# Moving one piece of the second feed-forward product ahead of a pair of products with V, and one subtraction up in VectorE's order

## The chip, the cores and the metric

The kernel runs on one core of a Trainium2 chip. A core has TensorE (PE, matmuls), VectorE (DVE), ScalarE (ACT), GpSimd (POOL) and SyncE (SP, which here issues all DMAs of the main loop). Each engine works through its own list of instructions in order and waits on semaphores for the others. The metric is the device time of the whole kernel in microseconds.

## The reference

The input is x with 4 sequences of 2048 tokens and 512 features. Two blocks follow each other, each with a residual:

```
h  = layernorm(x)
xk, xv, xr, xg = h + (h shifted by one token - h) * time_maa_{k,v,r,g}
r, k, v = xr @ Wr.T, xk @ Wk.T, xv @ Wv.T      # 32 heads of 16
g = silu(xg @ Wg.T)
for every chunk of 64 tokens:
    att   = (r @ k) * w_mat                      # 64 x 64 for every head
    y     = att @ v + (r @ state) * wb
    state = ws * state + (k * wk) @ v
x1  = x + (groupnorm(y) * gamma + beta) * g @ Wo.T
out = x1 + (gelu(layernorm(x1) @ W0.T + bias0) @ W1.T + bias1)   # hidden size 2048
```

## The kernel before

A prologue transposes the weights and splits each into a high and a low float16 part. Products of two split operands take three passes (high*high, high*low, low*high). "hi" parts are made by ScalarE as a float16 copy, "lo" parts by subtraction, mostly on VectorE.

The main loop runs over 32 blocks of 256 tokens. One step n of the loop mixes three stages of different blocks, so that TensorE always has something to do: attention of block n (`att_n`), gate, output product Wo and residual of block n-1 (`tail`), and the feed-forward layer of block n-2 (`ff`). The last four pieces of the second feed-forward product of block n-3 (`late`) stand in the next step. `ahead` is the normalizing and mixing of block n+1. Each engine has one function a step (`pe_step`, `dve_step`, `act_step`, `pool_step`, `sp_step`) with the order written out by hand.

The functions that matter here:

- `pe_down(eng, f, j)` (L785) is piece j of eight of the second feed-forward product: 8 matmuls of 128x512 that add into both banks of `F`. It waits for its weights in slot `use % 5` of `ring`, which `sp_weights` (L1291) loads; a load waits until the piece five uses back has been read.
- `pe_att_v(eng, n, t)` (L685) multiplies the attention weights of a pair of chunks with V, 96 small matmuls. It waits for `s_al`, which `dve_weights_lo` (L948) raises. `pe_from_state(eng, n, t)` (L702) follows.
- `pe_scores` (L669) makes the raw weights of chunk c, `dve_weigh` (L942) multiplies them with the decay mask, `act_weights_hi` (L1145) makes the high part, `dve_weights_lo` (L948) the low part.
- `mix_lo(eng, n, m)` (L234) makes the low part of mixed input m: 128x1024 elements, both inputs in SBUF. It waits for `act_mix_hi` (L230).
- `dve_state` (L957 and L971, in the last chunk L959) updates the state S; ScalarE copies it (L1151) and GpSimd makes its low part (L1257).
- `dve_variance` (L885) sums squares; `dve_residual` (L914) adds x to the output product in `B`, after which TensorE may write `B` again (`pe_Wo` for the second half, L753, waits for the first residual).
- `dve_take_y` (L987, L992) takes the pair's result out of the banks that `pe_att_v` and `pe_from_state` filled. `pe_V` (L639) of the next step waits for it and for `mix_lo` of input 2.

Within a step TensorE's order near the change is `pe_Wo` 0, `pe_kv`, `pe_down` 0, `pe_scores` 3, `pe_down` 1, `pe_Wo` 1, `pe_att_v` 1, `pe_from_state` 1, `pe_down` 2 and 3; the next step begins with `pe_K` (L611 into `sc`).

Of the kernel before, what the change touches and what calls it, by code (L numbers as in the profile page):

```python
# [34 lines left out]
def due(count):  # L35

    return not isinstance(count, int) or count > 0
# [29 lines left out]
def rows(t):  # L67
    return slice(P * t, P * t + P)
# [6 lines left out]
def program(nc, ctx, a, consts, x, out, wd, nb):  # L75
# [156 lines left out]
    def mix_lo(eng, n, m):  # L232
        eng.wait_ge(s_mh, 4 * n + m + 1)
        eng.tensor_tensor(mix[:, m % 2, 1, :, :], mixf[:, m % 2, :, :], mix[:, m % 2, 0, :, :],  # L234
                          ALU.subtract).then_inc(s_ml, 1)
# [364 lines left out]
    def in_step(n):  # L600

        return n < nb, 1 <= n <= nb, 2 <= n <= nb + 1, n + 1 < nb, 3 <= n <= nb + 2
# [12 lines left out]
    def pe_mixed(eng, n, m):  # L615
        eng.wait_ge(s_ml, 4 * n + m + 1)
        eng.wait_ge(s_mh, 4 * n + m + 1)

    def pe_K(eng, n, half):
        if due(n):  # L620
            eng.wait_ge(s_am, 8 * (n - 1) + 7 + half)
        pe_project_T(eng, sc[:, half, :], K_, n, 0, half).then_inc(s_pK, 1)
# [118 lines left out]
    def pe_Wo(eng, n, t):  # L741
        p = n - 1
        if t == 0:
            if n < nb:
                eng.wait_ge(s_gT, 2 * n + 2)
            if due(p):
                eng.wait_ge(s_x1, NT * p)
        else:
            eng.wait_ge(s_x1, NT * p + 1)
        eng.wait_ge(s_ygl, NT * p + t + 1)  # L750
        for i, (a, b) in enumerate(PASSES):
            for kk in range(G):
                mm = eng.matmul(B[:, :], yg[:, a, kk, rows(t)], WT[:, O_, b, kk, :],  # L753
                                start=(i == 0 and kk == 0), stop=(i == 2 and kk == G - 1))
        mm.then_inc(s_Wo, 1)
# [20 lines left out]
    def pe_down(eng, f, j):  # L776
        use = UNITS * f + 8 + j
        eng.wait_ge(s_w[use % RING], 16 * (use // RING + 1))
        if j == 0:
            eng.wait_ge(s_h, NH * (f + 1))  # L780
        for i in range(2):
            k = 2 * j + i
            for t in range(NT):
                for a in range(2):
                    mm = eng.matmul(F[:, t, :], hT[:, k, rows(t)], ring[:, use % RING, i, a * C:(a + 1) * C],  # L785
                                    start=(k == 0 and a == 0), stop=(k == NH - 1 and a == 1))
        mm.then_inc(s_dn, 1)

    def pe_step(eng, n):
        att_n, tail, ff, ahead, late = in_step(n)  # L790
        if att_n:
            pe_mixed(eng, n, 0)
            pe_K(eng, n, 0)
        if late:
            pe_down(eng, n - 3, 4)
        if att_n:
            pe_K(eng, n, 1)
        if late:
            pe_down(eng, n - 3, 5)
        if att_n:  # L800
            pe_mixed(eng, n, 1)
            pe_R(eng, n, 0)
        if late:
            pe_down(eng, n - 3, 6)
        if att_n:
            pe_R(eng, n, 1)
        if late:
            pe_down(eng, n - 3, 7)
        if att_n:
            pe_mixed(eng, n, 2)  # L810
            pe_V(eng, n, 0)
        if ff:
            pe_up(eng, n, 0)
        if att_n:
            pe_V(eng, n, 1)
        if ff:
            pe_up(eng, n, 1)
        if tail:
            pe_yT(eng, n)
        if ff:  # L820
            pe_up(eng, n, 2)
        if ahead:
            eng.wait_ge(s_rl, 2 * n + 1)
            pe_X(eng, n + 1, 0)
            eng.wait_ge(s_rl, 2 * n + 2)
            pe_X(eng, n + 1, 1)
        if ff:
            pe_up(eng, n, 3)
        if att_n:
            pe_scores(eng, n, 0)  # L830
            pe_kv(eng, n, 0, ahead)
            pe_G(eng, n, 0, ahead)
        if ff:
            pe_up(eng, n, 4)
        if att_n:
            pe_scores(eng, n, 1)
        if ff:
            pe_up(eng, n, 5)
        if att_n:
            pe_G(eng, n, 1, ahead)  # L840
        if ff:
            pe_up(eng, n, 6)
        if att_n:
            pe_att_v(eng, n, 0)
            pe_from_state(eng, n, 0)
            pe_scores(eng, n, 2)
        if ff:
            pe_up(eng, n, 7)
        if tail:
            pe_Wo(eng, n, 0)  # L850
        if att_n:
            pe_kv(eng, n, 1, ahead)
        if ff:
            pe_down(eng, n - 2, 0)
        if att_n:
            pe_scores(eng, n, 3)
        if ff:
            pe_down(eng, n - 2, 1)
        if tail:
            pe_Wo(eng, n, 1)  # L860
        if att_n:
            pe_att_v(eng, n, 1)
            pe_from_state(eng, n, 1)
        if ff:
            pe_down(eng, n - 2, 2)
            pe_down(eng, n - 2, 3)


# [68 lines left out]
    def dve_weigh(eng, n, c):  # L937
        for x in range(2):
            eng.wait_ge(s_sc, 8 * n + 2 * c + x + 1)
            if due(8 * n + 2 * c - 1 + x):  # L940
                eng.wait_ge(s_al, 8 * n + 2 * c - 1 + x)
            eng.tensor_tensor(att32[:, x, :], sc[:, x, :], wmask[:, 8 * x:8 * x + 8, :].rearrange("p q i -> p (q i)"),  # L942
                              ALU.mult).then_inc(s_am, 1)

    def dve_weights_lo(eng, n, c):
        for x in range(2):
            eng.wait_ge(s_ah, 8 * n + 2 * c + x + 1)
            eng.tensor_tensor(att[:, c % 2, 1, C * x:C * x + C], att32[:, x, :], att[:, c % 2, 0, C * x:C * x + C],  # L948
                              ALU.subtract).then_inc(s_al, 1)
# [70 lines left out]
    def dve_step(eng, n):  # L1020
        att_n, tail, ff, ahead, late = in_step(n)
        if not att_n:
            dve_e(eng, n - 3)
        for k in range(LN_STEPS):
            if ahead:
                dve_ln(eng, n + 1, k)
            if att_n:
                if k < 4:
                    dve_mix(eng, n, 2, k)
                elif k in (6, 13):  # L1030
                    dve_K_lo(eng, n, (6, 13).index(k))
                if 7 <= k < 11:
                    dve_mix(eng, n, 3, k - 7)
            if tail and k < 2 + RSQRT_STEPS + NT:
                dve_normalize(eng, n - 1, k)
        if att_n:
            mix_lo(eng, n, 2)
            dve_R_lo(eng, n, 0)
            dve_R_lo(eng, n, 1)
            if late:  # L1040
                dve_e(eng, n - 3)
            dve_vw(eng, n, 0)
            if ahead:
                dve_carry(eng, n + 1)
            eng.tensor_scalar(wsf[:, :], ws[:, :], flag[:, n + 1:n + 2], None, ALU.mult).then_inc(s_wsf, 1)
            dve_V_lo(eng, n, 0)
            mix_lo(eng, n, 3)
            dve_vw(eng, n, 1)
            dve_V_lo(eng, n, 1)
        if tail:  # L1050
            dve_gated(eng, n - 1)
        if ahead:
            dve_dx(eng, n + 1)
        if att_n:
            dve_weigh(eng, n, 0)
            dve_state(eng, n, 0)
            dve_weights_lo(eng, n, 0)
            dve_gate(eng, n, 0)
            dve_weigh(eng, n, 1)
            if ahead:  # L1060
                for g in range(2):
                    dve_mix(eng, n + 1, 0, g)
            dve_weights_lo(eng, n, 1)
            if ahead:
                for g in range(2, G):
                    dve_mix(eng, n + 1, 0, g)
            dve_state(eng, n, 1)
            if ahead:
                mix_lo(eng, n + 1, 0)
            dve_gate(eng, n, 1)  # L1070
            if ahead:
                for g in range(G):
                    dve_mix(eng, n + 1, 1, g)
            dve_take_y(eng, n, 0)
            dve_weigh(eng, n, 2)
            dve_weights_lo(eng, n, 2)
            dve_variance(eng, n, 0)
        if ahead:
            mix_lo(eng, n + 1, 1)
        if tail:  # L1080
            dve_residual(eng, n - 1, 0)
        if att_n:
            dve_state(eng, n, 2)
            dve_weigh(eng, n, 3)
            dve_weights_lo(eng, n, 3)
            dve_state(eng, n, 3)
        if tail:
            dve_residual(eng, n - 1, 1)
            dve_fln(eng, n - 1)
        if att_n:  # L1090
            dve_take_y(eng, n, 1)
# [376 lines left out]
```

## Time and profile before

| | |
|---|---|
| median of 3 runs | 2341.43 us (2336.86 to 2341.84) |
| profiled execution | 2341.74 us, span of its instructions 2339.9 us |
| mean granted TensorE clock | 0.962 of full |
| busy: TensorE / VectorE / ScalarE / GpSimd | 93% / 80% / 46% / 16% |

In the profile's rows a line such as "L685" is a line of the kernel; "x96" means 96 instructions merged into one row; what stands in square brackets is the idle time of that engine before the row and what ended it. Rows of instructions carry the start and the time in microseconds, counted from the start of the span. Merged rows overlap a little at their ends, since matmuls are pipelined; differences of starts are exact.

### The profile page before, as it was taken

The page shows a single profiled execution, that of the slowest core. Times are in us where ns is not written, and L with a number is a line of the kernel's source. Part 1 is how long each engine was busy: PE and PEld are TensorE (multiplying, and loading weights), DVE is VectorE, ACT ScalarE, POOL GpSimd, SP SyncE. Part 2 cuts the span into 40 slices and gives each one's busy share as a digit, 9 for nine tenths or more (in the row PEclk, how much of TensorE's full clock was granted, in tenths as well). Part 3 has the DMA queues.
Part 4 walks back from the last instruction along what each step waited for, and adds up shares of the span by engine and source line. Part 5 has one row for each costly group of instructions (what it writes and reads, how often), then busy time and mean ns, then how long its engine had stood idle before and what let it go on. Part 6 is the DMA issues. An engine that isn't in the chain of part 4 may idle for free.

```text
span 2339.9 us, 63070 instructions
## 1 busy us (share of the span) xinstructions
PE 2175.4 (93%) x26328; PEld 1567.0 (67%) x26328; DVE 1865.5 (80%) x4326; ACT 1077.9 (46%) x1902; POOL 384.6 (16%) x334
## 2 busy tenths in 40 slices
PE   3567999999999999999999999999999999999998
PEld 3455777766676776667677666777766676776664
DVE  5879888878887887888788788888888888888751
ACT  5533545444444544444454444445444444454441
POOL 0111111111111111111111111111111111111120
PEclk8788999999999999999999999999999999999999
DMA  8531566665556666555676656566665556666566
GB/s 263 193 87 50 164 204 212 196 201 168 180 173 199 213 196 202 166 174 180 199 215 196 195 166 189 184 197 204 196 208 178 178 176 193 203 204 194 171 211 209
DMA packets 281708, 437.83 MB, mean 187 GB/s; under 512 B 124752, under 2 KB 157904, under 8 KB 281424
## 3 DMA queue, kind: packets, MB, share of 16 engines
q1 hardware_dynamic: 276512, 433.31, 59.7%
q8 instruction: 209, 3.42, 0.6%
q10 hardware_dynamic: 4912, 0.48, 0.2%
q14 instruction: 75, 0.61, 0.1%
HBM read 316.27 MB, written 25.17 MB: 146 GB/s over the span
## 4 chain that ended last, share of the span: by engine, by line
PE 62%; DVE 23%; issue 5%; ACT 5%; DMA 1%; SPq 0%; DVEq 0%; POOL 0%; POOLq 0%; ACTq 0%
PE F L785 15%; PE F L771 13%; PE B L611 7%; PE Y L639 7%; PE sc L611 6%; DVE mixf L202 6%; DVE att L948 5%; PE T L611 3%; DVE mix L234 3%; PE Y L685 3%; DVE S L971 3%; ACT hT L1179 2%; DVE kv L957 2%; PE Y L702 2%; ACT att L1145 2%
## 5 line engine op out<-in xcount | busy, mean ns | idle before, releaser
L771 PE MATMUL F<-xT,ring 128*128 128x256 f16 x4096 | 491.2, 274 | 6.5 <-DMA xT<-xh 5.3
L785 PE MATMUL F<-ring,hT 128*128 128x512 f16 x2048 | 493.5, 389 | 1.2 <-ACT hT L1179 1.2
L771 PEld LDWEIGHTS F<-xT,ring 128*128 128x128 f16 x4096 | 397.2, 98 | 69.3 <-issue 8.1
L785 PEld LDWEIGHTS F<-ring,hT 128*128 128x128 f16 x2048 | 197.0, 100 | 218.2 <-issue 27.6
L230 ACT ACTIVATE mix<-mixf 128x1024 f16<-128x1024 f32 x128 | 135.3, 1057 | 378.2 <-DVE mixf L202 194.6
L1179 ACT ACTIVATE hT<-F,b,f_rho 128x256 f16<-128x256 f32 x512 | 260.3, 562 | 45.4 <-PE F L771 45.3
L202 DVE SCALAR_TENSOR_TENSOR mixf<-dx,maa,xnT 128x256 f32<-128x256 f32 x512 | 273.1, 559 | 0.0
L611 PE MATMUL B<-mix,WT 128*128 128x256 f16 x2304 | 269.5, 274 | 1.8 <-DVE gT L978 1.8
L1257 POOL TENSOR_TENSOR Shl<-S,Shl 128x512 f16<-128x512 f32 x128 | 153.9, 1202 | 691.4 <-ACT Shl L1151 691.4
L611 PEld LDWEIGHTS B<-mix,WT 128*128 128x128 f16 x2304 | 223.7, 98 | 37.9 <-DVE gT L978 2.0
L948 DVE TENSOR_TENSOR att<-att 128x512 f16<-128x512 f32 x256 | 179.8, 742 | 50.1 <-ACT att L1145 50.1
L1151 ACT ACTIVATE Shl<-S 128x512 f16<-128x512 f32 x128 | 80.1, 626 | 287.5 <-PE Y L702 145.7
L639 PE MATMUL Y<-WT,mix 128*128 128x512 f16 x768 | 178.9, 384 | 7.6 <-DVE mix L234 7.6
L611 PE MATMUL sc<-mix,WT 128*128 128x256 f16 x1536 | 180.3, 275 | 3.5 <-PEq L455 3.5
L1262 POOL TENSOR_TENSOR x<-e,x 128x512 f32<-128x512 f16 x64 | 73.0, 1161 | 671.8 <-DVE e L1017 671.8
L234 DVE TENSOR_TENSOR mix<-mixf,mix 128x1024 f16<-128x1024 f32 x126 | 181.6, 1441 | 0.0
L942 DVE TENSOR_TENSOR att<-sc,wmask 128x512 f32<-128x512 f32 x256 | 164.2, 683 | 20.7 <-PE sc L669 20.7
L753 PE MATMUL B<-WT,yg 128*128 128x512 f16 x768 | 178.6, 382 | 1.6 <-DVE x L914 1.5
L685 PE MATMUL Y<-vbd,att 128*64 128x32 f16 x6144 | 116.5, 187 | 63.1 <-DVE att L948 63.1
L611 PEld LDWEIGHTS sc<-mix,WT 128*128 128x128 f16 x1536 | 151.3, 99 | 35.0 <-issue 4.0
L685 PEld LDWEIGHTS Y<-vbd,att 128*64 128x64 f16 x6144 | 111.0, 118 | 84.3 <-issue 84.3
L1145 ACT ACTIVATE att<-att 128x512 f16<-128x512 f32 x256 | 148.5, 630 | 20.7 <-DVE att L942 19.6
(153 smaller groups left out, 2947.7 us busy)
## 6 DMA issues: line engine op xcount, KB each, us to landing
ring<-w_dram SPq DMA_DIRECT2D x512, 512.0 KB, 4.1
kx<-kT SPq DMA_DIRECT2D x96, 256.0 KB, 3.7
rx<-rT SPq DMA_DIRECT2D x96, 256.0 KB, 3.4
xa<-in_L_attn_x SPq DMA_DIRECT2D x32, 512.0 KB, 7.3
vbd<-vN SPq DMA_DIRECT2D x256, 64.0 KB, 2.7
x<-in_L_attn_x SPq DMA_DIRECT2D x32, 512.0 KB, 4.9
out<-x SPq DMA_DIRECT2D x32, 512.0 KB, 3.3
raw<-in_L_ffn_W SPq DMA_DIRECT2D x8, 1024.0 KB, 14.4
```

Source lines behind the costliest of these rows:

```text
L202: last = eng.scalar_tensor_tensor(out=mixf[:, m % 2, g, :], in0=dx[:, g, :], scalar=maa[:, m, g:g + 1], in1=xnT[:, g, 1:BT + 1], op0=ALU.m ...
L234: eng.tensor_tensor(mix[:, m % 2, 1, :, :], mixf[:, m % 2, :, :], mix[:, m % 2, 0, :, :], ALU.subtract).then_inc(s_ml, 1)
L611: mm = eng.matmul(out[:, gg * BT:(gg + 1) * BT], WT[:, w, a, kk, rows(g)], mix[:, m % 2, b, kk, :], start=(i == 0 and kk == 0), stop=(i == ...
L639: mm = eng.matmul(Y[:, t, :], mix[:, 0, a, kk, rows(t)], WT[:, V_, b, kk, :], start=(i == 0 and kk == 0), stop=(i == 2 and kk == G - 1))
L685: mm = eng.matmul(Y[Q * cc:Q * cc + Q, 0, 2 * N * q:2 * N * (q + 1)], att[:, cc, a, Q * q:Q * q + Q], vbd[:, t, cc, b, :, N * q:N * q + N] ...
L753: mm = eng.matmul(B[:, :], yg[:, a, kk, rows(t)], WT[:, O_, b, kk, :], start=(i == 0 and kk == 0), stop=(i == 2 and kk == G - 1))
L771: mm = eng.matmul(F[:, j % 2, i * BT:(i + 1) * BT], ring[:, use % RING, i, a * C + kk * P:a * C + (kk + 1) * P], xT[:, :, kk, :], start=(k ...
L785: mm = eng.matmul(F[:, t, :], hT[:, k, rows(t)], ring[:, use % RING, i, a * C:(a + 1) * C], start=(k == 0 and a == 0), stop=(k == NH - 1 a ...
L942: eng.tensor_tensor(att32[:, x, :], sc[:, x, :], wmask[:, 8 * x:8 * x + 8, :].rearrange("p q i -> p (q i)"), ALU.mult).then_inc(s_am, 1)
L948: eng.tensor_tensor(att[:, c % 2, 1, C * x:C * x + C], att32[:, x, :], att[:, c % 2, 0, C * x:C * x + C], ALU.subtract).then_inc(s_al, 1)
L1145: eng.activation(att[:, c % 2, 0, C * x:C * x + C], att32[:, x, :], ACT.Copy).then_inc(s_ah, 1)
L1179: eng.activation(hT[:, k, :], F[:, j % 2, i * BT:(i + 1) * BT], ACT.Gelu, bias=b0[:, k:k + 1], scale=f_rho[:, 0:1]).then_inc(s_h, 1)
```

## The change

On TensorE, `pe_down(n - 2, 2)` goes from behind `pe_from_state(n, 1)` to a place ahead of `pe_att_v(n, 1)`. On VectorE, `mix_lo(n + 1, 1)` goes from behind `dve_variance(n, 0)` to a place ahead of `dve_weights_lo(n, 2)`. Nothing is added or removed.

```diff
@@ pe_step
         if tail:
             pe_Wo(eng, n, 1)
+        if ff:
+            pe_down(eng, n - 2, 2)
         if att_n:
             pe_att_v(eng, n, 1)
             pe_from_state(eng, n, 1)
         if ff:
-            pe_down(eng, n - 2, 2)
             pe_down(eng, n - 2, 3)
@@ dve_step
             dve_take_y(eng, n, 0)
             dve_weigh(eng, n, 2)
+        if ahead:
+            mix_lo(eng, n + 1, 1)
+        if att_n:
             dve_weights_lo(eng, n, 2)
             dve_variance(eng, n, 0)
-        if ahead:
-            mix_lo(eng, n + 1, 1)
         if tail:
             dve_residual(eng, n - 1, 0)
```

## Rows read from the trace of the kernel before

**Rows 1.** The waits of the whole span: engine, line, releaser: us, times, longest.

```profile
PE Y L685 <- DVE att L948: 63.1, 33, 7.5
```

**Rows 2.** Timeline of TensorE in step 16: start, us, instruction, [idle before].

```profile
1224.13 1.90 PE L785 MATMUL F<-ring,hT 128*128 128x512 f16 x8
1225.87 2.75 PE L753 MATMUL B<-WT,yg 128*128 128x512 f16 x12
1230.42 2.17 PE L685 MATMUL Y<-vbd,att 128*64 128x32 f16 x96 [1.79 <-DVE att L948]
...
1233.82 4.05 PE L785 MATMUL F<-ring,hT 128*128 128x512 f16 x16
1237.71 2.78 PE L611 MATMUL sc<-mix,WT 128*128 128x256 f16 x24
...
1255.09 2.75 PE L639 MATMUL Y<-WT,mix 128*128 128x512 f16 x12
```

**Rows 3.** Timeline of TensorE, the same place in four other steps.

```profile
276.86 1.70 PE L685 MATMUL Y<-vbd,att 128*64 128x32 f16 x96 [1.19 <-DVE att L948]
...
1435.26 1.70 PE L685 MATMUL Y<-vbd,att 128*64 128x32 f16 x96 [1.51 <-DVE att L948]
...
1441.04 1.15 PE L611 MATMUL sc<-mix,WT 128*128 128x256 f16 x9
...
1502.04 1.70 PE L685 MATMUL Y<-vbd,att 128*64 128x32 f16 x96 [1.79 <-DVE att L948]
...
2182.40 1.94 PE L685 MATMUL Y<-vbd,att 128*64 128x32 f16 x96 [1.78 <-DVE att L948]
```

**Rows 4.** Timeline of TensorE in step 31, the last with attention.

```profile
2246.07 2.75 PE L753 MATMUL B<-WT,yg 128*128 128x512 f16 x12
2248.75 1.70 PE L685 MATMUL Y<-vbd,att 128*64 128x32 f16 x96
```

**Rows 5.** Stretches: span, busy by engine, then granted clock, DMA share, GB/s.

```profile
1230.40:1234.00 3.60, 3.58 (x121) 3.38 (x122) 3.53 (x8) 0.06 (x1) 0.00 (x0) 0.62 0.02 5
1436.80:1441.00 4.20, 4.20 (x50) 2.26 (x44) 3.87 (x14) 0.63 (x1) 1.15 (x1) 1.00 0.13 29
```

**Rows 6.** Timeline of VectorE in step 16 and the start of step 17.

```profile
1219.03 1.28 DVE L942 TENSOR_TENSOR att<-sc,wmask 128x512 f32<-128x512 f32 x2
1221.77 1.29 DVE L948 TENSOR_TENSOR att<-att 128x512 f16<-128x512 f32 x2 [1.46 <-ACT att L1145]
...
1223.57 1.22 DVE L234 TENSOR_TENSOR mix<-mixf,mix 128x1024 f16<-128x1024 f32 x1
1224.70 0.75 DVE L914 SCALAR_TENSOR_TENSOR x<-B,out_scale,x 128x512 f32<-128x512 f32 x1
...
1237.73 0.69 DVE L987 TENSOR_TENSOR yi<-Y,wb 128x512 f32<-128x512 f32 x1
...
1249.39 1.22 DVE L234 TENSOR_TENSOR mix<-mixf,mix 128x1024 f16<-128x1024 f32 x1
1250.53 0.68 DVE L872 SCALAR_TENSOR_TENSOR rT<-B,rT 128x512 f16<-128x512 f32 x1
1255.20 0.69 DVE L872 SCALAR_TENSOR_TENSOR rT<-T,rT 128x512 f16<-128x512 f32 x1 [3.99 <-ACT rT L1097]
```

**Rows 7.** Timeline of ScalarE in step 16, then GpSimd in step 16.

```profile
1217.82 1.06 ACT L230 ACTIVATE mix<-mixf 128x1024 f16<-128x1024 f32 x1 [2.55 <-DVE mixf L202]
...
1220.38 1.16 POOL L1257 TENSOR_TENSOR Shl<-S,Shl 128x512 f16<-128x512 f32 x1 [9.97 <-ACT Shl L1151]
```

**Rows 8.** Timelines of VectorE and GpSimd in step 17, where both read SBUF.

```profile
1259.97 2.13 DVE L234 TENSOR_TENSOR mix<-mixf,mix 128x1024 f16<-128x1024 f32 x1
...
1259.86 1.16 POOL L1271 TENSOR_TENSOR vw<-vw 128x512 f16<-128x512 f32 x1 [0.95 <-ACT vw L1123]
```

**Rows 9.** SyncE's DMA queue in step 16, then the page's row of landings.

```profile
1201.66 7.92 SPq L1291 DMA_DIRECT2D ring<-w_dram  x3
...
ring<-w_dram SPq DMA_DIRECT2D x512, 512.0 KB, 4.1
```

## The prediction

> **What bounds the kernel now.** The first view read is the page's shares of busy time: TensorE is busy 93% of the span, the next engine, VectorE, 80%. That alone would make TensorE's work the bound and leave little to win. The view of waits shows where its remaining idle time lies: one wait dominates, 63.1 us in 33 times, TensorE at the second pair of products with V for the low part of the attention weights [rows 1]. The timeline of TensorE then shows one step in order. In step 16 the second half of Wo starts at 1225.87 and the products with V at 1230.42, 4.55 us later [rows 2]. In step 31 the same two rows lie 2.68 us apart, with no wait between them [rows 4]. So the hole costs 1.87 us, a little more than the 1.79 us of idle time that the row names. The hole is there once in each of the steps 2 to 30. Everywhere else in a middle step TensorE's rows follow each other.
>
> The hole has a second price. After it, in step 16, the two groups and the two pieces of the feed-forward product take 7.29 us until the next step's K product (1230.42 to 1237.71) [rows 2], while around 1435 they take 5.78 us (1435.26 to 1441.04) [rows 3]. The granted clock tells why: 0.62 on average in the stretch behind the hole in step 16, so part of it at 1.2 GHz, and 1.00 in the step at 1436.80 [rows 5]. The instructions are the same. The clock falls in most steps, always right behind the hole, but not in all of them: from 1435.26 to 1502.04 a period takes 66.78 us with the hole and at full clock, while the 28 periods from 276.86 to 2182.40 take 68.05 us on average [rows 3].
>
> **What VectorE does meanwhile.** It is what TensorE waits for. From the weighing of chunk 2 to the weights of chunk 3 it is dense, but for 1.46 us in which it waits for ScalarE's high part (1220.31 to 1221.77) [rows 6]. Behind the critical stretch it has room again: 3.99 us of waiting for ScalarE's high part of R [rows 6].
>
> **The first edit: `pe_down` 2 into the hole.** It adds no work. One piece is 8 matmuls and takes 1.74 us from start to start (piece 1, 1224.13 to 1225.87) [rows 2], so of the 5.78 us at full clock the V and state products make 5.78 - 2 x 1.74 = 2.3. With the piece moved, TensorE comes to the V products at 1225.87 + 2.68 + 1.74 = 1230.29. Even with VectorE as late as before, the weights are there at 1230.42 less the time of a semaphore. So the piece fills 1.74 of the 1.87 us by itself, and the rest needs 0.13 us from the second edit. The wait that the moved piece brings along is that for its weights. The third of three loads that SyncE issues in 1201.66 to 1209.58 is this one (its slot comes free with `pe_up` 5), and a load lands 4.1 us after its issue [rows 9]: at about 1213.7, 15 us before it is wanted. SyncE's next load, which waits for this piece, is released earlier by the move. The hidden values are complete before `pe_down` 0.
>
> **The second edit: `mix_lo` into VectorE's idle time.** Its input is ready: ScalarE's copy is done at 1218.88 (1217.82 + 1.06) [rows 7]. Alone the subtraction takes 1.13 us from start to start (1223.57 to 1224.70), and the idle time is 1.46 us [rows 6]. In the best case all of it vanishes and everything from the residual to the weights of chunk 3 comes 1.13 us earlier. But GpSimd's low part of S runs from 1220.38 for 1.16 us, in just this idle time [rows 7], and the two do not get along: in step 17 the same subtraction starts 0.11 us after a GpSimd operation of 1.16 us and takes 2.13 us in place of 1.22 [rows 6, 8]. If the moved one is stretched like that, it holds VectorE until about 1220.23 + 2.05 = 1222.28, the weights of chunk 2 start 0.51 us later than before, and 0.62 us of the gain remain. If it is GpSimd that is pushed back and then disturbs the weights of chunk 2, 0.91 us are lost in place of 0.51 and 0.22 us remain. I take 0.6 us, since the case in step 17 is nearest, and keep 0.2 and 1.13 as the ends. GpSimd's result itself is wanted only by the state update some 3 us later.
>
> The Trainium skill ("SBUF — State Buffer", Who interferes with whom) states the rule against this move: a VectorE instruction with two inputs in SBUF contends with a GpSimd instruction that reads SBUF, and who issues first decides who is held. By this rule the moved subtraction, which would start first, delays GpSimd, which is my lower end; the 2.13 us in step 17 agree with it, as there GpSimd was first.
>
> **What is late next.** In the numbers of step 16 the weights of chunk 3 are ready at 1230.42 - 0.6 = 1229.8, and TensorE arrives at 1230.29: no wait, with 0.5 us to spare (0.1 at the lower end, 1.0 at the upper). The next step's K product then starts at 1230.29 + 5.78 - 1.74 = 1234.33 in place of 1237.71, 3.38 us earlier, while VectorE is only 0.6 us earlier. Two places decide whether it follows. Its wait of 3.99 us for the high part of R shrinks to 3.99 - 3.38 + 0.6 = 1.2 us; the end of R's low part, the eviction of `F` and the feed-forward start thus keep their distance to TensorE. Its `mix_lo` of input 2 ends at 1250.61 - 0.6 and the V product will want it at 1255.09 - 3.38 = 1251.7: 1.7 us of room [rows 2, 6]. Lastly `dve_take_y` 1 stands behind the layernorm statistics and starts at 1237.73, now 1237.1; the state product that it reads ends at 1230.29 + 2.3 = 1232.6, so putting a piece ahead of it costs nothing [rows 2, 6]. SyncE's loads are all released by TensorE's own progress.
>
> **The sum.** Holes: 28 of 1.87 us (steps 3 to 30) and one of 1.26 in step 2 (its row shows 1.19 of idle, by the same difference of 0.07 to 0.08) [rows 3]: 53.6 us. Clock: 28 periods from 276.86 to 2182.40 are 1905.54 us, at 66.78 they would be 1869.84, so 35.7 us; behind the hole of step 30, if the clock falls there as in step 16, another 7.29 - 5.78 = 1.5: 37.2 us in all. This comes back whole only if no hole is left for the clock to fall behind. In steps 0 and 1 there is no feed-forward piece to move and VectorE waits for little; I count them as nothing, plus or minus 1 us. The sum is 90.8 us. The profiled execution took 2341.74 us, so 2250.9; it lies 0.3 us above the median of the runs. A middle period becomes 66.78 - 1.87 = 64.9 us. I predict 2251 us.
>
> **The rivals.**
> *The clock falls all the same.* Of the gain of 90.8 us only the 53.6 us of the holes come: 2288 us. For it speaks that the clock did not fall behind every hole of the same length, so the hole is not the whole condition. Against it: it never fell in a place without the hole in the rows read, and in step 31, without the hole, the V products ran at full pace (1.70 us, as at 1435.26) [rows 3, 4]. The Trainium skill ("TensorE: Matmul & The Clock Gate", HAM oscillation) makes idle gaps much longer than this one the cause of such falls; by that rule a hole of 1.79 us would not be the cause, and 2288 us would come out. The trace speaks otherwise, as the falls stand right behind the hole.
> *VectorE stays the bound.* The collision with GpSimd costs more than reckoned, or ScalarE falls in between, so that VectorE gains nothing or loses some tenths. From a loss of 0.2 to 0.5 us a hole of about 0.3 to 0.6 us remains in each of 29 steps, 9 to 18 us, and in some steps the clock falls behind it (up to 15 us more): 2260 to 2284 us, say 2268. For it: the reserve of 0.5 us is less than the 0.9 us of one collision. Against it: the low end of my bounds still hides it.
> *The change does nothing.* The idle time moves: the hole reappears before the next step's V product, for the low part of input 2. That needs VectorE to be 1.7 us later at that place than I reckon, and all gain to be lost it must be 3.4 + 1.1 us later; 2341 us.
> *Slower.* TensorE stands at the moved piece for its weights, with the V products and the state product behind it, and VectorE's `dve_take_y` behind those. That decides from a landing later than about 1228.5 + 3.4 us, against 1213.7 [rows 9]; a landing at 1234 would cost 2 us a step, 2341 + 60 = 2400 us. The room is 18 us.
>
> **How the numbers follow.** My forecast (2246 to 2257 us: bounds of steps 0 and 1, and a few periods with a small hole) gets 0.70, VectorE as the bound 0.14, the clock falling all the same 0.07, no effect 0.04, slower 0.05. Two runs of this kernel differ by about 0.2%, which is what can be told from no change. The forecast and the next two rivals are all faster: 0.91; same 0.04, slower 0.05. The range reaches from 2244 us to 2280 us, which takes in most of the second case and leaves out the third.
>
> **What would show it.** In the profile after: no wait of TensorE on L948 behind L753 in the middle steps, or one below 0.2 us; V products of 1.70 us in every step; a period of 64.9 us; a mean granted clock above 0.98; VectorE's row of L234 at about 1220.2 of its step between 1.2 and 2.2 us long, and its wait on L872 near 1.2 us. TensorE's share of busy time nears 97%. I am wrong if the wait on L948 remains with over half a microsecond, if a wait on L639 for L234 shows in middle steps, or if TensorE's rows become longer with the clock below 1.00 where no idle time stands ahead of them.

## The result and the profile after

The changed kernel takes 2250.97 us (median of 4 runs, 2250.44 to 2251.30) against 2341.24 us: ratio 0.9618 (ratios are of the means), 95% interval 0.9601 to 0.9635. The forecast was 2251 us. One execution of `e7_late2` below fell in a slower state of the chip, 2905.19 us at a mean granted clock of 0.716, and its ratio leaves it out. The profiled execution of the changed kernel took 2250.65 us, its span is 2248.8 us and its mean granted TensorE clock 0.980, against 0.962. Behind the edits line numbers have shifted: by one on VectorE (L948 is now L949) and by two on ScalarE and GpSimd (L1257 is now L1259).

Three of the waits of TensorE over the whole span of the changed kernel: engine, line, releaser, us in total, times, longest. The others lie in the prologue, in steps 0 and 1 and at the end, or are gaps of at most 0.4 us in the middle.

```profile
PE Y L685 <- DVE att L949: 11.0, 4, 7.5
PE Y L639 <- DVE mix L234: 9.0, 2, 6.6
PE F L771 <- DMA xT<-xh: 5.7, 2, 3.0
```

The wait at the products with V fell from 63.1 us in 33 times [rows 1] to 11.0 us in 4, and those four lie in steps 0 and 1, where there is no feed-forward piece to put into a hole. No other wait has taken its place: the two of 9.0 us and the two of 5.7 us are those of the first steps and of the last ones.

TensorE's timeline around the same place in the changed kernel, and the products with V one step later:

```profile
1176.74 0.69 PE L669 MATMUL sc<-rx,kx 64*64 64x64 f16 x32
1177.37 1.90 PE L785 MATMUL F<-ring,hT 128*128 128x512 f16 x8
1179.10 2.75 PE L753 MATMUL B<-WT,yg 128*128 128x512 f16 x12
1181.69 1.89 PE L785 MATMUL F<-ring,hT 128*128 128x512 f16 x8
1183.51 1.70 PE L685 MATMUL Y<-vbd,att 128*64 128x32 f16 x96
1185.06 0.84 PE L702 MATMUL Y<-Shl,rT 128*64 128x128 f16 x24
1185.83 1.90 PE L785 MATMUL F<-ring,hT 128*128 128x512 f16 x8
1187.56 2.78 PE L611 MATMUL sc<-mix,WT 128*128 128x256 f16 x24
...
1248.43 1.70 PE L685 MATMUL Y<-vbd,att 128*64 128x32 f16 x96
```

From Wo to the products with V it is 4.41 us with a useful piece between them, where it was 4.55 us with a hole [rows 2]. Behind it every row has its short form, and the K product of the next step follows after 4.05 us. A period is 1248.43 - 1183.51 = 64.92 us. The stretch of the middle says the same in both kernels (span, then busy us of TensorE, weight loads, VectorE, ScalarE and GpSimd, then the granted clock, DMA share, GB/s), first of the kernel before:

```profile
300.00:2100.00 1800.00, 1754.00 (x21657) 1266.38 (x21655) 1487.23 (x3447) 844.51 (x1491) 310.60 (x267) 0.98 0.62 192
```

and of the changed kernel:

```profile
300.00:2100.00 1800.00, 1798.94 (x22714) 1300.80 (x22713) 1573.02 (x3615) 878.47 (x1556) 349.23 (x278) 1.00 0.64 200
```

TensorE has 1.06 us of idle time left in 1800, at full clock.

VectorE in the same step of the changed kernel:

```profile
1172.26 1.28 DVE L943 TENSOR_TENSOR att<-sc,wmask 128x512 f32<-128x512 f32 x2
1173.45 1.21 DVE L234 TENSOR_TENSOR mix<-mixf,mix 128x1024 f16<-128x1024 f32 x1
1174.99 1.84 DVE L949 TENSOR_TENSOR att<-att 128x512 f16<-128x512 f32 x2 [0.33 <-ACT att L1147]
1176.76 0.67 DVE L886 TENSOR_REDUCE gn_s<-yi 128x32 f32<-128x512 f32 x1
1177.35 0.73 DVE L915 SCALAR_TENSOR_TENSOR x<-B,out_scale,x 128x512 f32<-128x512 f32 x1
...
1179.78 1.28 DVE L943 TENSOR_TENSOR att<-sc,wmask 128x512 f32<-128x512 f32 x2
1181.22 1.70 DVE L949 TENSOR_TENSOR att<-att 128x512 f16<-128x512 f32 x2 [0.16 <-ACT att L1147]
1182.84 0.74 DVE L960 SCALAR_TENSOR_TENSOR kv<-Y,flag,headmask 128x512 f32<-128x512 f32 x1
...
1190.18 0.69 DVE L988 TENSOR_TENSOR yi<-Y,wb 128x512 f32<-128x512 f32 x1
...
1205.06 0.69 DVE L873 SCALAR_TENSOR_TENSOR rT<-T,rT 128x512 f16<-128x512 f32 x1 [1.40 <-ACT rT L1099]
```

and GpSimd beside it:

```profile
1173.61 2.07 POOL L1259 TENSOR_TENSOR Shl<-S,Shl 128x512 f16<-128x512 f32 x1 [9.96 <-ACT Shl L1153]
```

The subtraction fills 1.13 us of what were 1.46 us of waiting; 0.33 us are left. It began before GpSimd's operation and kept its own 1.21 us. GpSimd paid, 2.07 us in place of 1.16 [rows 7], and its late end then stretched the pair of weights of chunk 2, 1.84 us in place of 1.29 [rows 6]. From the weighing to the residual it is now 5.09 us, where it was 5.67 [rows 6]: VectorE gained 0.58 us. The weights of chunk 3 end at 1181.22 + 1.70 = 1182.92, and TensorE comes to them at 1183.51.

### The profile page after: what moved, and what is told of

Its sections match the earlier page's. It is cut to its first block, busy times and chain, and to the rows that moved or that the text cites. A ratio compares the mean times of both kernels' runs of the same rounds, so it can differ in the third digit from the quotient of the medians.

```text
span 2248.8 us, 63070 instructions
## 1 busy us (share of the span) xinstructions
PE 2132.4 (95%) x26328; PEld 1540.3 (68%) x26328; DVE 1880.4 (84%) x4326; ACT 1075.0 (48%) x1902; POOL 411.9 (18%) x334
## 4 chain that ended last, share of the span: by engine, by line
PE 90%; DVE 3%; issue 1%; DMA 1%; ACT 0%; POOL 0%; POOLq 0%; SPq 0%; ACTq 0%; DVEq 0%
PE F L771 20%; PE F L785 20%; PE B L611 11%; PE Y L639 7%; PE B L753 7%; PE sc L611 7%; PE Y L685 4%; PE T L611 3%; PE sc L669 3%; PE T L726 2%; PE Y L702 2%; PE sc L652 1%; DVE mixf L202 1%; PE B L241 1%; PE T L241 1%
## 5 line engine op out<-in xcount | busy, mean ns | idle before, releaser
L785 PE MATMUL F<-ring,hT 128*128 128x512 f16 x2048 | 482.1, 380 | 1.3 <-ACT hT L1181 1.2
L1259 POOL TENSOR_TENSOR Shl<-S,Shl 128x512 f16<-128x512 f32 x128 | 180.6, 1411 | 644.4 <-ACT Shl L1153 644.4
L949 DVE TENSOR_TENSOR att<-att 128x512 f16<-128x512 f32 x256 | 195.7, 803 | 17.9 <-ACT att L1147 17.9
L639 PEld LDWEIGHTS Y<-WT,mix 128*128 128x128 f16 x768 | 75.7, 99 | 95.4 <-DVE mix L234 9.5
L753 PEld LDWEIGHTS B<-WT,yg 128*128 128x128 f16 x768 | 75.4, 99 | 89.3 <-issue 3.6
```

The source lines that it names most:

```text
L639: mm = eng.matmul(Y[:, t, :], mix[:, 0, a, kk, rows(t)], WT[:, V_, b, kk, :], start=(i == 0 and kk == 0), stop=(i == 2 and kk == G - 1))
L1259: eng.tensor_tensor(Shl[:, b, 1, :], S[:, :], Shl[:, b, 0, :], ALU.subtract).then_inc(s_Sl, 1)
```

## The experiments

The kernel before was run beside each of them. Its medians there were 2336.4 to 2339.6 us, so ratios are given too.

**Each edit alone.** `e1_piece_only` is the changed kernel without this hunk, `e2_mix_only` the kernel before with this hunk alone:

```diff
+        if ahead:
+            mix_lo(eng, n + 1, 1)
+        if att_n:
             dve_weights_lo(eng, n, 2)
             dve_variance(eng, n, 0)
-        if ahead:
-            mix_lo(eng, n + 1, 1)
```

> The changed kernel with the subtraction put back in its old place: only the feed-forward piece is moved. Theory (the piece fills 1.74 of the 1.87 us of the hole, the weights of chunk 3 come as late as before): a hole of about 0.13 us is left in 29 steps, too short for the clock to fall, so 2251 + 4 = 2255 us. Rival A (the subtraction's earlier place carries part of the gain): its 0.58 us a step are missing, 2251 + 17 = 2268 us. Rival B (a hole of any length brings the clock down): 2255 + 37 = 2292 us.

Measured: 2255.04 us, ratio 0.9631 (0.9609 to 0.9653). Its timeline of TensorE:

```profile
1184.07 2.75 PE L753 MATMUL B<-WT,yg 128*128 128x512 f16 x12
...
1188.61 1.69 PE L685 MATMUL Y<-vbd,att 128*64 128x32 f16 x96
1190.13 0.86 PE L702 MATMUL Y<-Shl,rT 128*64 128x128 f16 x24
...
1253.65 1.70 PE L685 MATMUL Y<-vbd,att 128*64 128x32 f16 x96
```

From Wo to the V products 4.54 us in place of 4.41, a period of 65.04 us: the hole of 0.13 us that was reckoned, at full clock. The two kernels' intervals overlap, so the difference in time is not shown by the runs, only by the rows.

> The kernel before with only the subtraction moved up. Theory: the weights of chunk 3 come 0.58 us earlier in each of 29 steps, the hole shrinks from 1.87 to about 1.3 us and the period by as much: 2341 - 17 = 2324 us, if the clock still falls behind the shorter hole as often. Rival A (a hole of 1.2 us as in step 2 is too short for the clock to fall): 2341 - 17 - 37 = 2287 us. Rival B (the collision with GpSimd eats the gain): 2341 us.

Measured: 2286.11 us, ratio 0.9760 (0.9740 to 0.9781). This is rival A, not what I expected. Its timeline of TensorE:

```profile
1197.88 2.75 PE L753 MATMUL B<-WT,yg 128*128 128x512 f16 x12
1201.84 1.70 PE L685 MATMUL Y<-vbd,att 128*64 128x32 f16 x96 [1.20 <-DVE att L948]
1203.36 0.87 PE L702 MATMUL Y<-Shl,rT 128*64 128x128 f16 x24
```

The hole is 0.59 us shorter (3.96 us from row to row in place of 4.55). That is worth 17 us in 29 steps. But the granted clock is 1.00 from 250 to 2150 us, and this is worth the rest: the V and state products have their short forms. An edit that gives VectorE 0.58 us a step brings over half of the whole gain when it is alone.

**The clock by itself.** `e3_fill` is the kernel before with useless work in the hole:

```diff
+    def pe_fill(eng, n):
+        eng.wait_ge(s_km, NCH * n + 3)
+        for i in range(8):
+            eng.matmul(T32[:, :], WT[:, O_, 0, i % 4, 0:P], WT[:, O_, 0, i % 4, :], start=True, stop=True)
...
         if att_n:
+            if ff:
+                pe_fill(eng, n)
             pe_att_v(eng, n, 1)
```

> The kernel before with eight matmuls of 128x512 that compute nothing wanted (weights with weights into a free bank) in front of the second products with V, in the steps with a feed-forward stage: the hole stays as long for the useful work, but TensorE is busy in it. Theory (the idle hole brings the clock down): the V products start where they did, every row runs at full clock, 2341 - 37 = 2304 us. Rival (the clock falls for another reason, such as the mix of small matmuls behind the hole): 2341 us or more.

Measured: 2306.86 us, ratio 0.9855 (0.9835 to 0.9874), against 2304 expected. Its timeline of TensorE (L792 is the added work):

```profile
1207.95 2.75 PE L753 MATMUL B<-WT,yg 128*128 128x512 f16 x12
1210.54 1.89 PE L792 MATMUL T<-WT 128*128 128x512 f16 x8
1212.50 1.70 PE L685 MATMUL Y<-vbd,att 128*64 128x32 f16 x96
1214.02 0.86 PE L702 MATMUL Y<-Shl,rT 128*64 128x128 f16 x24
```

The products with V come 4.55 us behind Wo, exactly as before; only the clock differs. 240 added matmuls a run, of no use, make the kernel 1.4% faster. So the idleness in the hole caused the fall of the clock. By the medians the fall cost 32 us. The rows say a little more. The 28 periods of the middle take 1873.81 us (275.30 to 2149.11) in place of 1905.54, 31.7 us less. But five of them are 0.5 to 1.1 us longer than 66.78, 4.0 us in all, each with a gap for which the profile shows no engine that TensorE waited for ("issue"), such as this one:

```profile
997.88 1.70 PE L771 MATMUL F<-xT,ring 128*128 128x256 f16 x14 [1.09 <-issue]
```

Without these gaps it is 35.7 us, the forecast's figure for the 28 periods.

**More in front of the V products.** `e4_two_pieces` also moves `pe_down(eng, n - 2, 3)` ahead of them.

> The changed kernel with piece 3 of the feed-forward product also moved ahead of the second products with V. Theory (VectorE takes the pair's result only at 1190.18 of step 16, the state product would end at about 1187.6, so there is room): no change, 2251 us, within 2 us. Rival (whatever is put ahead of the V products delays VectorE, the mechanism of my slower case): up to 1.74 us a step, 2251 + 50 = 2301 us.

Measured: 2250.61 us, ratio 0.9611 (0.9589 to 0.9633): no difference from the change. Its timeline of TensorE, then of VectorE (L987 takes the pair's result):

```profile
1182.10 2.75 PE L753 MATMUL B<-WT,yg 128*128 128x512 f16 x12
1184.69 3.62 PE L785 MATMUL F<-ring,hT 128*128 128x512 f16 x16
1188.23 1.70 PE L685 MATMUL Y<-vbd,att 128*64 128x32 f16 x96
1189.78 0.84 PE L702 MATMUL Y<-Shl,rT 128*64 128x128 f16 x24
```

```profile
1193.32 0.69 DVE L987 TENSOR_TENSOR yi<-Y,wb 128x512 f32<-128x512 f32 x1
```

The state products end 8.5 us behind the start of Wo in place of 6.8, and VectorE still comes 2.7 us after their end, when the layernorm statistics are done. What was put ahead of the V products costs nothing.

**The collision with GpSimd.** `e5_pool_later` lets GpSimd wait:

```diff
         b = (c + 1) % 2
+        if c == 1:
+            eng.wait_ge(s_al, 8 * n + 6)
         eng.tensor_tensor(Shl[:, b, 1, :], S[:, :], Shl[:, b, 0, :], ALU.subtract).then_inc(s_Sl, 1)
```

> The changed kernel, in which GpSimd's low part of S of chunk 1 also waits for the low parts of the weights of chunk 2, so that it no longer runs beside the two subtractions on VectorE. Theory (two operations that read two tensors of SBUF hold each other up): GpSimd's operation takes 1.16 us in place of 2.07, VectorE's pair of weights of chunk 2 takes 1.3 in place of 1.84, the weights of chunk 3 come another 0.5 us earlier; the time stays at 2251 us, as TensorE does not wait for them. Rival (VectorE is still the bound somewhere in the step): 29 x 0.5 = 15 us less, 2236 us.

Measured: 2251.48 us, ratio 0.9637 (0.9607 to 0.9668). Its VectorE, then its GpSimd:

```profile
1174.30 1.28 DVE L943 TENSOR_TENSOR att<-sc,wmask 128x512 f32<-128x512 f32 x2
1175.49 1.21 DVE L234 TENSOR_TENSOR mix<-mixf,mix 128x1024 f16<-128x1024 f32 x1
1177.04 1.29 DVE L949 TENSOR_TENSOR att<-att 128x512 f16<-128x512 f32 x2 [0.33 <-ACT att L1147]
...
1184.33 0.74 DVE L960 SCALAR_TENSOR_TENSOR kv<-Y,flag,headmask 128x512 f32<-128x512 f32 x1
```

```profile
1178.48 1.16 POOL L1261 TENSOR_TENSOR Shl<-S,Shl 128x512 f16<-128x512 f32 x1 [12.79 <-DVE att L949]
```

Apart, both operations have their old lengths again, and from the weighing of chunk 2 to the state update it is 10.03 us in place of 10.58. So the collision costs VectorE 0.55 us a step, and the kernel nothing: the time does not move.

**How much room there is, and which hole brings the clock down.** In the changed kernel VectorE gets instructions that nobody uses, in the steps with a feed-forward stage (1, 2, 4 or 5 of them in the runs, four in the hunk below; in `e10_late4half` four and one of half the size):

```diff
             dve_weigh(eng, n, 3)
+            if ff:
+                for i in range(4):
+                    eng.bn_stats(pad[:, i, :], wmask[:, 0:8, :].rearrange("p q i -> p (q i)"))
             dve_weights_lo(eng, n, 3)
```

> The changed kernel with one idle VectorE instruction (statistics of a constant tile, 0.6 us from start to start) behind the weighing of chunk 3, in 30 steps. Theory (0.59 us lie between the end of the weights of chunk 3 and the V products, less 0.14 us for the semaphore, so 0.45 us to spare): a hole of 0.15 us, too short for the clock: 2251 + 4 = 2255 us. Rival A (the room is larger than it looks): 2251. Rival B (any hole brings the clock down): 2292 us.

> The same with two idle instructions, 1.2 us. Theory: a hole of 0.75 us in 30 steps, 22 us; the clock does not fall behind so short a hole: 2273 us. Rival (the clock falls behind it): up to 2310 us.

> The same with four idle instructions, 2.4 us. Theory: a hole of 1.95 us in 30 steps, 58 us, and the clock falls behind it as in the kernel before, 37 us more: 2346 us. Rival A (the piece that was moved keeps the clock up through the hole): 2309 us. Rival B (VectorE's own lateness is not absorbed behind the hole, at its wait for the high part of R of 1.40 us): more than 2360 us.

> The changed kernel with five idle VectorE instructions behind the weighing of chunk 3. With four the pair of weights ended 1.80 us later and the wait shown was 1.20 us at full clock; a fifth makes the wait 1.80 us, as long as in the kernel before. Theory (the length of the idle hole decides over the clock): 0.6 us more in 30 steps, 2290 + 18 = 2308 us, and the clock falls behind most holes as in the kernel before, 37 us more: 2345 us, granted clock in the middle about 0.98. Rival (the clock fell for what stood in the hole's surroundings before the piece was moved): 2308 us at full clock.

> The same with four idle instructions and one of half the size (about 0.33 us): a wait of about 1.53 us, between the one that kept the clock (1.20) and the one that lost it (1.79). Theory: 2290 + 10 = 2300 us at full clock, up to 2337 if the clock falls behind every hole as before; in between if it falls behind some.

| | added | wait shown | period at full clock | granted clock, 300 to 2100 us | median us (ratio, interval) |
|---|---|---|---|---|---|
| changed kernel | 0 | none | 64.92 | 1.00 | 2250.97 (0.9618, 0.9601 to 0.9635) |
| e6_late1 | 1 | none | 64.91 | 1.00 | 2253.23 (0.9642, 0.9616 to 0.9668) |
| e7_late2 | 2 | none | 65.00 | 1.00 | 2255.01 (0.9649, 0.9618 to 0.9680) |
| e8_late4 | 4 | 1.20 | 66.17 | 1.00 | 2289.82 (0.9801, 0.9774 to 0.9829) |
| e10_late4half | 4.5 | 1.52 | 66.50 | 0.99 | 2312.31 (0.9881, 0.9846 to 0.9917) |
| e9_late5 | 5 | 1.79 | 66.78 | 0.98 | 2334.76 (0.9983, 0.9964 to 1.0003) |

The first instruction costs VectorE nothing at all, a surprise. In `e6_late1` its rows are:

```profile
1185.93 1.28 DVE L944 TENSOR_TENSOR att<-sc,wmask 128x512 f32<-128x512 f32 x2
1187.13 0.68 DVE L1090 BATCH_NORM_STATS2 pad<-wmask 128x6 f32<-128x512 f32 x1
1187.73 1.34 DVE L950 TENSOR_TENSOR att<-att 128x512 f16<-128x512 f32 x2
1188.99 0.74 DVE L961 SCALAR_TENSOR_TENSOR kv<-Y,flag,headmask 128x512 f32<-128x512 f32 x1
```

From the weighing of chunk 3 to the state update 3.06 us pass, as in the changed kernel (1179.78 to 1182.84). The added one fills the wait of 0.16 us for ScalarE, and the pair of weights, which starts 0.4 us later, meets only the last 0.2 us of GpSimd's operation on S and takes 1.34 us in place of 1.70:

```profile
1186.76 1.16 POOL L1263 TENSOR_TENSOR Shl<-S,Shl 128x512 f16<-128x512 f32 x1 [4.92 <-ACT Shl L1157]
```

In the changed kernel this operation starts at 1180.61, before the pair at 1181.22, so this second collision of the step stretches VectorE's pair and not GpSimd's operation. From the second instruction on the sum holds: two instructions make VectorE 0.53 us late and the hole 0.08 us long, four make it 1.71 us late and the period 1.25 us longer. So the room is 0.45 us, as expected for `e6_late1`; the prediction had 0.5. My expectations for these runs had left out the first instruction's free ride, and so came out 18 us too high for two and, together with the clock, 56 us too high for four.

The clock is the second finding. TensorE in `e8_late4`, with a wait of 1.20 us:

```profile
1202.03 1.70 PE L686 MATMUL Y<-vbd,att 128*64 128x32 f16 x96 [1.20 <-DVE att L950]
1203.54 0.86 PE L703 MATMUL Y<-Shl,rT 128*64 128x128 f16 x24
```

and in `e9_late5`, with 1.79 us:

```profile
1222.72 1.82 PE L686 MATMUL Y<-vbd,att 128*64 128x32 f16 x96 [1.79 <-DVE att L950]
1224.33 1.51 PE L703 MATMUL Y<-Shl,rT 128*64 128x128 f16 x24
1225.78 2.74 PE L786 MATMUL F<-ring,hT 128*128 128x512 f16 x8
```

The last one is the kernel before over again: same wait, same slow rows behind it, same time (0.9983). Of its 28 middle periods 20 are about 68.3 us long and 8 are 66.78; in the kernel before 22 are long. With 1.52 us 10 of 28 are long: nine of about 68.1 us in place of 66.50, and one of 70.03, whose first rows are slow (2.01 us below) and which also holds a gap of 0.39 us in which TensorE waited for nothing that the profile shows. With 1.20 us none is long for the clock: 25 of 28 are 66.17 to 66.20 us, one is 66.59, and two (67.56 and 67.77) hold a gap of 1.19 and of 1.43 us of the same kind, with the rows around it at their short forms. In `e2_mix_only`, with the same wait of 1.20 us, the 27 periods from 341 us on are all 66.17 to 66.20. The tenth long period of `e10_late4half` begins so:

```profile
1817.68 2.01 PE L686 MATMUL Y<-vbd,att 128*64 128x32 f16 x96 [1.52 <-DVE att L950]
```

So the last 0.6 us of waiting cost 45 us by the medians (43 by the ratios), of which 18 are the waiting itself.

## Why the prediction was right

**The hole and its two prices.** Both terms of the sum were right, 53.6 us for the holes and 37.2 for the clock: a period lost the hole's length, and `e3_fill` gave 35.7 us of the clock's share back in the 28 middle periods by itself. A middle period was forecast at 64.9 us and is 64.92. From step 2 to step 30 the 28 periods fell from 1905.54 to 1819.63 us (273.94 to 2093.57 in the changed kernel), 85.9 us of the 88.1 in my sum for them; the missing 2 us lie in six periods of 65.1 to 65.5 us. No wait for another engine is shown in them; three hold a gap of 0.17 to 0.40 us of the "issue" kind. Where these gaps come from is open. Against that, and in no term of the sum, the changed kernel's profiled execution reached the first V products of step 0 at 133.77 in place of 135.73, behind matmuls at a clock still rising. So the agreement to the microsecond is partly luck; the mechanism is not.

**The piece in the hole.** It was to fill 1.74 of 1.87 us by itself, with 0.13 left: `e1_piece_only` shows 0.13. Its weights were there and nothing waited for the state products, as `e4_two_pieces` shows with twice as much in front of them.

**The subtraction.** The size was right (0.6 us taken, 0.58 measured), the mechanism was not the one that I held nearest. I took the case in which GpSimd is first and the subtraction takes 2.13 us [rows 8]. In fact VectorE was first, as the start times before had shown, GpSimd was held, and the pair behind was stretched: my lower case, which cost 0.55 us and not the 0.91 that I had set for it. The rule of the Trainium skill ("SBUF — State Buffer", Who interferes with whom), that the one who issues first holds the other up, gave the right order; that the held one then disturbs the next instruction as well is in the rows of this case.

**The rooms behind.** The weights of chunk 3 were to have 0.5 us to spare: 0.45 by the padded runs. The wait for the high part of R was to shrink to 1.2 us and is 1.40. No wait for the low part of input 2 came up in the middle. Only TensorE's share of busy time missed: 95% of the whole span, not near 97%. The old busy time over the new span would have been 97%, but the busy time fell too, from 2175.4 to 2132.4 us: the slow rows behind the hole had counted as busy, and they became short. In the middle the share is above 99.9%.

**The rivals.** The clock falling all the same: refuted by `e3_fill`, which takes away the idleness and nothing else. The rule of the Trainium skill ("TensorE: Matmul & The Clock Gate", HAM oscillation), which makes idle gaps much longer than this one the cause, does not cover this case: behind the wait of 1.79 us in step 16 the mean granted clock was 0.62 [rows 5]. VectorE as the bound: it did not come, with 0.45 us a step to spare; it begins with the second added instruction, by 0.08 us. No effect and slower: nothing in the runs speaks for them.

**What the two edits are worth.** They are not added up: the piece alone brings 86 us, the subtraction alone about 55, both 90. Each alone is enough to keep the clock, and that part can be won only once. In the forecast I had given the subtraction the rest of the hole and nothing else; that is its worth behind the piece, not by itself.

No run beats the changed kernel by more than the runs scatter. TensorE is full in the middle, so another order of the same work has little left to win there; this was argued from the rows, and not tried beyond the two orders above.

## What to carry to other kernels

Price a short stall on TensorE with what follows it: look whether the rows behind it are longer than the same rows elsewhere, and how many periods are of either length; here the clock was 37 of 90 us. If the stall can't be filled with useful work, shortening it a little, or filling it with useless matmuls into a free bank, can bring most of this part. And before a subtraction is moved into VectorE's idle time, look what GpSimd does just then, and whether anyone waits for the result of either.

## What the runs showed of the hardware

- The granted clock fell behind idle waits of 1.79 us (22 of 28 periods in the kernel before, 20 of 28 in `e9_late5`), behind fewer of 1.52 us (10 of 28 in `e10_late4half`) and behind none of 1.20 us (`e8_late4` and `e2_mix_only`, both at a mean of 1.00). Falls follow one another: in `e9_late5` the periods that end in steps 5 to 11 are all short and those that end in steps 12 to 30 all long. What decides between a fall and none for the same wait was not tried.
- Eight useless matmuls of 128x512 in the hole were enough to keep it at 1.00 (`e3_fill`).
- Two operations that each read two tensors of SBUF, one on VectorE and one on GpSimd: the one that started first kept its time (1.21 us), the other grew from 1.16 to 2.07 us and stretched the next pair on VectorE from 1.29 to 1.84 us.
- An instruction more on VectorE cost nothing, since a wait of 0.16 us and most of a collision with GpSimd fell away for it: 3.06 us with it and without it (`e6_late1`).
